# Layer norm, dilated attention and feed-forward on one core: in the front, the second segment's rows are loaded and normalised later, and three weight remainders change engine or place

## The reference, cut to what matters

```python
# x (16, 1024, 256) fp32, H = 16 heads of 16, SEG = 512, DIL = 8, BLOCK_M = 64
xn = _layernorm(x, axis=-1)
q, k, v = xn @ Wqkv.T                    # q scaled by 1/4
k4, v4 = k, v of every 8th row of a segment of 512 rows
scores = q4 @ k4.T                       # per head and segment: 512 x 64
c = max of scores over the 64 rows of a block, per key
w = exp(scores - c); out = (w @ v4) / (sum_k w + 1e-10)
attention = out @ Wout.T
ffn = relu(xn @ W1 + b1) @ W2 + b2       # 256 -> 1024 -> 256
return x + attention + ffn
```

## Time and profile before

| | us |
|---|---|
| median of 3 runs | 1069.88 |
| lowest and highest run | 1069.55, 1072.47 |
| the profiled execution, its time | 1070.42 |
| its span, first to last instruction | 1068.6 |
| granted TensorE clock, mean over the span | 0.999 of full |

### The profile page before, as it was taken

The page is one execution under the profiler, slowest core; times in us unless marked ns, Lnnn a source line. Parts: engine busy times, 40 slices in busy tenths (PEclk is TensorE's granted clock), DMA queues, the critical chain, the costliest instruction groups (busy, mean ns, idle before and its releaser), DMA issues.

```text
span 1068.6 us, 19173 instructions
## 1 busy us (share of the span) xinstructions
PE 1046.8 (98%) x5381; PEld 811.4 (76%) x5381; DVE 817.3 (76%) x1465; ACT 648.3 (61%) x1080; POOL 622.3 (58%) x487
## 2 busy tenths in 40 slices
PE   6999999999999999999999999999999999999998
PEld 4677787777787777777777877777877777877777
DVE  7877877877878777778778778778777778787753
ACT  5656665666656566565666656666666665656663
POOL 4355565656656656556655656566565565556564
PEclk9999999999999999999999999999999999999999
DMA  5457777777776878777777777778778687767744
GB/s 192 98 155 210 223 213 207 195 213 220 223 213 179 224 201 232 221 195 198 207 223 223 215 208 197 217 214 229 213 192 216 197 236 212 211 175 218 194 144 145
DMA packets 153576, 216.38 MB, mean 202 GB/s; under 512 B 27344, under 2 KB 96720, under 8 KB 153552
## 3 DMA queue, kind: packets, MB, share of 16 engines
q1 hardware_dynamic: 153408, 215.96, 72.5%
q10 hardware_dynamic: 144, 0.13, 0.0%
HBM read 100.41 MB, written 58.46 MB: 149 GB/s over the span
## 4 chain that ended last, share of the span: by engine, by line
PE 84%; DMA 6%; DVE 4%; SPq 3%; issue 2%; ACT 0%; DVEq 0%
PE h_bank L1023 36%; PE y_bank L1023 36%; PE s_banks L1096 5%; PE misc L1203 3%; PE s_banks L1203 2%; DMA k_dram<-k_lo 2%; PE misc L1023 2%; DMA yt_dram<-y_mem 1%; DVE xn L824 1%; DMA xt_dram<-z 1%; DMA k_pack<-k_dram 1%; SPq L406 1%; DVE s_max L841 1%; SPq L428 1%; DMA x_raw<-x 1%
## 5 line engine op out<-in xcount | busy, mean ns | idle before, releaser
L533 POOL TENSOR_TENSOR h_lo<-h_full,h_hi 128x512 fp32r<-128x512 f32 x256 | 336.1, 1314 | 382.2 <-ACT h_full L614 378.8
L620 ACT ACTIVATE w_exp<-w_exp 128x512 f32<-128x512 f32 x256 | 161.6, 632 | 241.8 <-DVE w_exp L847 240.2
L612 ACT ACTIVATE h_hi<-h_bank,b_cols 128x512 fp32r<-128x512 f32 x256 | 174.5, 682 | 70.2 <-PE h_bank L1023 63.4
L1023 PE MATMUL h_bank<-xt_hi,w_hi 128*128 128x512 f32 x512 | 206.4, 403 | 0.0
L1023 PE MATMUL h_bank<-xt_lo,w_hi 128*128 128x512 f32 x512 | 200.2, 391 | 0.0
L1023 PE MATMUL h_bank<-xt_hi,w_lo 128*128 128x512 f32 x512 | 199.7, 390 | 0.0
L841 DVE TENSOR_REDUCE s_max<-s_banks 128x8 f32<-128x512 f32 x254 | 170.9, 673 | 34.5 <-PE s_banks L1096 34.5
L1023 PE MATMUL y_bank<-h_hi,w_hi 128*128 128x512 f32 x496 | 194.7, 392 | 0.2 <-ACT w_exp L620 0.2
L1023 PE MATMUL y_bank<-h_lo,w_hi 128*128 128x512 f32 x496 | 193.9, 391 | 0.0
L1023 PE MATMUL y_bank<-h_hi,w_lo 128*128 128x512 f32 x496 | 193.6, 390 | 0.0
L847 DVE TENSOR_TENSOR w_exp<-s_banks,s_max 128x512 f32<-128x512 f32 x254 | 175.7, 692 | 11.0
(11 more groups left out here) (139 smaller groups left out, 1509.4 us busy)
## 6 DMA issues: line engine op xcount, KB each, us to landing
q_pack<-q_hi SPq DMA_DIRECT2D x248, 128.0 KB, 2.5
rden_rows<-rden_dram SPq DMA_DIRECT2D x128, 128.0 KB, 4.6
x_b<-x SPq DMA_DIRECT2D x32, 512.0 KB, 4.5
x_raw<-x SPq DMA_DIRECT2D x31, 512.0 KB, 4.8
q_pack<-q_lo SPq DMA_DIRECT2D x124, 128.0 KB, 2.4
yt_dram<-y_mem SPq DMA_DIRECT2D x124, 128.0 KB, 3.6
y_mem<-yt_dram SPq DMA_DIRECT2D x31, 512.0 KB, 4.7
out<-x_b SPq DMA_DIRECT2D x31, 512.0 KB, 3.1
```

The lines of the kernel that those rows point to most:

```text
L533: pool.tensor_tensor(h_part[1][:, i % HBUF], h_full[:, i % HBUF], f32(h_part[0][:, i % HBUF]), ALU.subtract).then_inc(h_lo, 1)
L612: act.activation(h_part[0][:, i % HBUF], h_bank[i % 2][:], ACT.Relu, bias=b1_cols[:, i:i + 1]).then_inc(h_hi, 1)
L620: act.activation(w_exp[:, pair], w_exp[:, pair], ACT.Exp).then_inc(w_ready, 1)
L1023: mm = pe.matmul(ps, stationary[a], moving[b], start=start and c == 0 and n == 0, stop=stop and c == len(pairs) - 1 and n == 2, skip_group ...
```

## The change

- SP issues the rows of segment 1 behind wkv and wq instead of ahead of them.
- DVE takes the statistics of segment 1 (`statistics(1, 1)`, L771) behind `keys_projected_lo(-2, 0)` instead of ahead of `normalise_keys(0)`, the mean and variance right behind it, and `normalise(1, 1)` moves from the end of `first_step` into `lead_step`, ahead of pair 4.
- wq's remainder goes from DVE to POOL, with a wait for `xn_ready` 1.
- The second half of w2's remainder goes from DVE (ahead of pair 6) to POOL, between `hidden_lo(0, 2)` and `hidden_lo(0, 3)`. DVE waits for it at pair 6.
- POOL's wait for `xn_ready` 2 goes away; `inverse_deviation(1, 1)` moves behind w1 and the first half of w2.
- ACT makes `wq_hi` ahead of the first keys' `xkey_hi`.
- PE does `second_product(0, 1)` ahead of the transposes of segment 1.

```diff
@@ SP first_step
-                load_x(1, 1)
                 sp.dma_start(wkv_raw, wkv_t.rearrange("(c p) n -> p c n", p=P)).then_inc(wkv_loaded, 16)
                 sp.dma_start(wq_raw, wq_t.rearrange("(c p) n -> p c n", p=P)).then_inc(wq_loaded, 16)
+                load_x(1, 1)
@@ POOL first_step, lead_step
                 inverse_deviation(0, 0)
+                pool.wait_ge(xn_ready, 1)
+                pool.wait_ge(wq_hi, 1)
+                pool.tensor_tensor(wq[1][:], wq_raw, f32(wq[0][:]), ALU.subtract).then_inc(wq_lo, 1)
                 for half in range(2):
                     pool.wait_ge(w1_hi[half], 1)
-                    if half == 1:
-                        inverse_deviation(1, 1)
-                        pool.wait_ge(xn_ready, 2)
                     pool.tensor_tensor(w1_half(w1s[1], half), ...)
-                pool.wait_ge(w2_hi[0], 1)
-                pool.tensor_tensor(w2_half(w2s[1], 0), ...)
+                second_lo(0)
+                inverse_deviation(1, 1)
+            def second_lo(half):
+                pool.wait_ge(w2_hi[half], 1)
+                pool.tensor_tensor(w2_half(w2s[1], half), w2_half(w2_raw, half), f32(w2_half(w2s[0], half)),
+                                   ALU.subtract).then_inc(w2_lo[half], 1)
             def lead_step():
-                for i in range(4):
+                for i in range(3):
                     hidden_lo(0, i)
+                second_lo(1)
+                hidden_lo(0, 3)
                 hidden_lo(0, 4)
@@ ACT first_step
                 weight_hi(wkv_raw, wkv[0][:], wkv_loaded, 16, wkv_hi)
+                weight_hi(wq_raw, wq[0][:], wq_loaded, 16, wq_hi)
                 keys_hi(-2)
-                weight_hi(wq_raw, wq[0][:], wq_loaded, 16, wq_hi)
@@ DVE first_step
                 mean_variance(0, 0)
-                statistics(1, 1)
                 normalise_keys(0)
                 normalise(0, 0)
                 keys_lo(-2)
                 weight_lo(wkv_raw, wkv[0], wkv[1], wkv_hi, wkv_lo)
-                weight_lo(wq_raw, wq[0], wq[1], wq_hi, wq_lo)
                 transposed_lo(-2, 0)
                 drain_kv(-2)
-                statistics_done(1)
-                mean_variance(1, 1)
                 mask_k(-2)
                 queries_lo(-2, 0)
                 keys_projected_lo(-2, 0)
-                normalise(1, 1)
+                statistics(1, 1)
+                statistics_done(1)
+                mean_variance(1, 1)
@@ DVE lead_step
                     if n == 4:
+                        normalise(1, 1)
                         dve.wait_ge(w2_lo[0], 1)
                     if n == 6:
-                        weight_lo(w2_half(w2_raw, 1), w2_half(w2s[0], 1), w2_half(w2s[1], 1), w2_hi[1], w2_lo[1])
+                        dve.wait_ge(w2_lo[1], 1)
@@ PE lead_step
                 second_product(0, 0)
+                second_product(0, 1)
                 pe.wait_ge(s_shifted, 4)
                 transpose_x(-1, 1)
-                second_product(0, 1)
                 first_scores((6, 7), DH, 6)
```

More of the change, by code:

```diff
@@ L577, in first_step @@
                 inverse_deviation(0, 0)
+                pool.wait_ge(xn_ready, 1)
+                pool.wait_ge(wq_hi, 1)
+                pool.tensor_tensor(wq[1][:], wq_raw, f32(wq[0][:]), ALU.subtract).then_inc(wq_lo, 1)
                 for half in range(2):
                     pool.wait_ge(w1_hi[half], 1)
-                    if half == 1:
-                        inverse_deviation(1, 1)
-                        pool.wait_ge(xn_ready, 2)
                     pool.tensor_tensor(w1_half(w1s[1], half), w1_half(w1_raw, half), f32(w1_half(w1s[0], half)),
                                        ALU.subtract).then_inc(w1_lo[half], 1)
-                pool.wait_ge(w2_hi[0], 1)
-                pool.tensor_tensor(w2_half(w2s[1], 0), w2_half(w2_raw, 0), f32(w2_half(w2s[0], 0)),
-                                   ALU.subtract).then_inc(w2_lo[0], 1)
+                second_lo(0)
[4 more added lines that the diff above has]
+                                   ALU.subtract).then_inc(w2_lo[half], 1)
             def lead_step():
-                for i in range(4):
+                for i in range(3):
                     hidden_lo(0, i)
+                second_lo(1)
+                hidden_lo(0, 3)
                 hidden_lo(0, 4)
```

## The result

The changed kernel takes 1073.88 us (median of 11 runs, 1072.13 to 1078.5) against 1069.55 of the kernel before beside it (11 runs, 1066.78 to 1072.47): a ratio of 1.0045, 95% interval 1.0028 to 1.0061. It is slower by some 4 us. Measured again later, it took 1075.57 against 1069.88, a ratio of 1.0049 (1.0028 to 1.0070). The profiled execution took 1073.76.

What follows compares the result with a forecast made beforehand. TensorE, busy 98% of the span, was taken as the bound, so only its waits matter. Terms 1 and 2 are included in a 3.7 us loss from the collision, term 4 adds nothing: 1069.88 + 3.7 = 1073.6; range 1071.2 to 1077.0.

Steps and rivals of the forecast that it cites:

- Term 1: First normalisation: without segment 1's statistics ahead, segment 0 is normalised and TensorE's transposes begin 1.3 us earlier.
- Term 2: First scores: the early start is all given back waiting on w2's cast and k_lo, and 0.2 us more.
- the early start lives: Rival, front: w2 lands 1.2 us or more earlier, 1.3 reaches the scores; 1068.8 with the collision avoided; chance 0.06.
- Term 3: normalise(1, 1) on DVE waits for POOL's instructions: 3.5 us; scores of pairs 6 and 7 at 34.5, 3.7 lost in all.
- Term 4: Work taken off DVE (w2's half, wq's remainder) saves nothing; TensorE's swapped order costs and gains nothing by itself.
- The clock: Rival, TensorE between 30.2 and 34.5: clock falls too, some 6 us at half pace cost 3, giving 1076.6; chance 0.15.
- The sum: Whole kernel: median 1069.88 plus 3.7 gives 1073.6 us, chance 0.55.

Runs made afterwards that it cites:

- after_again: The changed kernel, unaltered, measured once more against the kernel before: 1075.57 us against 1069.88, ratio 1.0049.
- e4_move_alone: Kernel before with only normalise(1, 1) moved ahead of pair 4 and POOL's wait for xn_ready 2 removed; ratio 1.0038 to the kernel before.
- e5: Changed kernel with two more POOL waits: w1's second half for k_lo, hidden_lo(0, 2) for xn_ready 2; ratio 0.9995 to the kernel before.
- e1: Changed kernel with one more POOL wait: hidden_lo(0, 2) waits for xn_ready 2; ratio 1.0004 to the kernel before.
- e2: Changed kernel with the second half of w2's remainder back on DVE, ahead of pair 6; ratio 1.0013, again 1.0015, to the kernel before.
- e6_klo: Changed kernel with POOL's second half of w1's remainder waiting for k_lo, no wait for normalise; ratio 1.0060 to the kernel before.
- e3_fill: Changed kernel with 13 extra unread products on TensorE in its two waits; ratio 1.0064, again 1.0060, to the kernel before.
- e8_split: Changed kernel with POOL's second half of w2's remainder cut into four instructions 256 wide; ratio 1.0025 to the kernel before.

## Why the prediction was right, step by step

- **Term 1, 1.3 earlier: the right sign, 0.8 in size.** The statistics went out of the way, but segment 0's rows landed some 0.3 later in this execution; in `after_again` `xn` starts at 8.43, 1.6 earlier than before. wq's remainder held `wkv_lo` for 0.85 (2.07 less 1.22; forecast 0.6), and TensorE did wait 0.56 for `xt_lo` behind it, which I had called hidden. It cost nothing in the end, for the reason of term 2.
- **Term 2, all given back: right as a sum, wrong in its first step.** I had w2 land at 16.30 as before. It landed at 15.12, and `k_hi` was ready by 17.14. This was not one lucky execution: in the ten profiles with the new order of loads the cast of w2's first half starts between 14.76 and 16.15, in the two with the old order (before, e4_move_alone) at 16.30 and 16.09. So the condition of my rival "the early start lives", w2 1.2 earlier, was as good as met (1.18 in the changed kernel's profile). What gave the start back was `k_lo` alone: reached at 17.55, held by the second half of w1 until 18.49, done at 18.78. e5 shows what it would have been without (17.67); it meets that rival's other condition too, the collision avoided, and yet its ratio, 0.9995, is not clear of 1. The scores came 0.3 earlier, not 0.2 later.
- **Term 3, the collision: right.** Forecast ends of the four instructions 27.7, 30.1, 31.4, 31.8; measured 27.26, 29.67, 30.94 and 31.26, behind POOL instructions that ended at 27.11, 29.52 and 30.79. All four are 0.4 to 0.5 early because `k_lo` was done at 18.78 and not at 19.3 (term 2), and with it the first scores and the hidden tiles came sooner. The waits were 1.7 and 1.6 (forecast 1.65 and 1.85), the scores at 34.06 (34.5), a loss of 3.3 there (3.7). e1 shows that the loss in the front comes from POOL's instructions beside `xn` and from nothing else in the change, e2 that w2's half is the decisive one of them. With the rule of the Trainium skill (page "SBUF — State Buffer", section "Who interferes with whom"), an exclusive lock for whole instructions, the trace agrees: `k_lo`, which has two inputs in SBUF, took 1.23 instead of 0.42. That `xn`, with a single tensor input, is held as well, and that DVE gets exactly one instruction in between two of POOL's, is what the rows here show.
- **Term 4, nothing saved: right.** The freed 2.4 us of DVE never reached TensorE: `xt_lo` was done at 35.1, and the products that need it began at 40.48. That TensorE's own new order costs nothing was argued in the prediction and is not tested by a run.
- **The clock: mis-sized.** I gave it 0.15 as a rival beside the forecast. It fell in both profiles of the changed kernel, at the same place, and in that of e6_klo, which has both waits (2.98 and 1.62). It cost 2.3 there (5.6 late at the packed scores, 3.3 before them), where the rival had 3. By the mean clocks of the single runs it was there in 16 of 23 at most. The ground I gave against it, that the wait of 1.6 for `k_full` costs no clock, is false in other executions (e1_gate, e3_fill, e8_split).
- **The sum: 1073.6 against 1073.88.** In part by luck of two errors. The profiled front was 5.6 late, 2.3 of it the clock's, which the sum lacked; and the stretch behind it was 2.3 shorter than in the profile of before, where the waits for `k_pack` sum to 2.2 less (1.3 instead of 3.5), though one wait put down to "issue" between 800 and 1000 us is 0.9 longer. Over the 12 profiles the total for `k_pack` lies anywhere between 1.3 and 5.0 us, and follows no part of the change that I could name. The second measurement came to 5.7 over, 2.0 more than the forecast's 3.7, though its interval holds both.

## What to carry to other kernels

An elementwise operation moved from VectorE to GpSimd is not off VectorE if it stands beside VectorE's own work from SBUF to SBUF: with GpSimd's queue full, VectorE got one instruction in per GpSimd instruction, so a group of n short ones waits for up to n long ones. Not all of VectorE's work is held. Here it was the normalisation, the subtractions with both inputs in SBUF and a copy. The statistics, which read SBUF too, took 1.39 beside w2's first half on POOL, no more than the 1.41 before, and the shifts of scores, which read PSUM, kept their 0.69:

```profile
18.70 1.39 DVE L777 BATCH_NORM_STATS2 stats_second<-x_raw 128x6 f32<-128x256 f32 x4
```

Before removing a wait on GpSimd, ask what it kept apart, and which of VectorE's operations somebody waits for; a wait put back in front of the colliding instructions undid the loss here (1.0004). And price a wait opened on TensorE with the clock that may fall behind it.

## What the runs showed of the hardware that was not expected

- The granted clock fell to 1.2 GHz not only in the 4.4 us with eight transposes (33.1 to 39.9) but behind single waits: 1.64 for `k_full` (e1_gate, 55.9 to 59.4; e3_fill, 59.4 to 62.8; e8_split, 57.5 to 61.1), 1.73 for `k_pack` (e3_fill, 175.4 to 178.8), and 1.80 and 2.70 for `k_lo` (e8_split, 20.1 to 23.5; e4_move_alone, 20.6 to 24.0). The same wait of 1.64 is in all 12 profiles, and in nine the clock stayed full behind it; it stayed full behind 2.19 for `k_lo` in e1_gate too. Of 32 runs of the kernel before, made beside the first four experiments, 14 had a mean granted clock of 1.0 and took 1069.0 on average, and 10 had 0.998 and took 1070.9. None of the changed kernel's 23 runs was above 0.998.
- GpSimd loses a little too where VectorE slips in: w2's first half took 2.58 where the held `k_lo` ran beside its start, and 2.39 to 2.40 where it did not (before, e5_gate_and_klo, e6_klo). It took 2.54 in e4_move_alone, where `k_lo` was held as well but no statistics stood behind it.
